# A two-layer graph network: the message stage's end reordered, eight source columns fetched row by row, and three scatters of the sum stage stored row by row

## What is computed

```
# layer 0: attention over the incoming edges, 4 heads of 32
h = relu(layernorm(x)); e = (h @ W_embed)
logit = leaky(dot_src[src] + dot_dst[dst]);  prob = softmax of logit over the edges with one dst
x = x + segment_sum(e[src] * prob, dst) + h @ W_lin + bias
# layer 1: messages, summed at the SOURCE node
h = relu(layernorm(x))
m = relu([h[src], h[dst], edge_attr] @ W1 + b1) @ W2 + b2
x = x + segment_sum(m * sigmoid(edge_attr @ Wa + ba), src)
```

## Time and profile before

| | us |
|---|---|
| median of 3 runs | 1634.91 |
| the profiled execution | 1633.1 |
| its span | 1631.4 |
| rows stage | 0 to 679 |
| sums stage | 679 to 985 |
| messages stage | 985 to 1631 |

### The profile page before, as it was taken

How to read it: one execution, slowest core, us unless ns; L and a number is a source line. 1 busy time by engine, 2 the same in 40 slices (tenths; PEclk the granted TensorE clock), 3 DMA queues, 4 the chain that set the end, 5 groups by cost and what they waited for, 6 DMA issues and landing times.

```text
span 1631.4 us, 24533 instructions
## 1 busy us (share of the span) xinstructions
PE 1118.8 (69%) x6191; PEld 848.0 (52%) x6191; DVE 1168.5 (72%) x3895; ACT 775.7 (48%) x2040; POOL 1105.6 (68%) x985
## 2 busy tenths in 40 slices
PE   2577677677777777554446545977778798888864
PEld 1455455555555555444445443644556566556543
DVE  3777787777877877976878675865666687777752
ACT  2567777777777777554545441322222222222221
POOL 6266666666666663266666656778788888888875
PEclk9988988988888888666756756998999999999988
DMA  4366666665666665454545442333333333333332
GB/s 125 105 203 193 200 194 194 213 194 190 212 197 200 199 199 163 137 155 146 161 132 162 144 133 66 47 54 52 53 53 53 52 52 54 53 51 51 54 48 28
DMA packets 181797, 202.75 MB, mean 124 GB/s; under 512 B 24777, under 2 KB 134225, under 8 KB 181657
## 3 DMA queue, kind: packets, MB, share of 16 engines
q1 hardware_dynamic: 123711, 129.49, 24.5%
q0 software_dynamic: 56272, 71.16, 22.2%
q10 hardware_dynamic: 1674, 0.53, 0.2%
HBM read 90.62 MB, written 109.66 MB: 123 GB/s over the span
## 4 chain that ended last, share of the span: by engine, by line
DVE 33%; SPq 23%; issue 15%; PE 12%; another core or an unknown queue 9%; ACT 3%; POOL 3%; DMA 1%; ACTq 1%; DVEq 0%; POOLq 0%
SPq L1254 15%; DVE st L540 4%; DVE BD L578 4%; SPq L1252 4%; SPq L1253 3%; DVE H L972 3%; DVE st L545 3%; PE bank L854 2%; PE bank L870 2%; PE bank L867 2%; DVE BD L585 2%; DVE BD L554 2%; DVE BD L1017 2%; PE bank L873 2%
## 5 line engine op out<-in xcount | busy, mean ns | idle before, releaser
L1194 POOL DMA_INDIRECT out_dram<-BD,BS x196 | 203.9, 1040 | 144.9 <-DVE BD L1021 88.9
L1274 POOL DMA_INDIRECT XE<-out_dram,gidx x189 | 187.2, 991 | 60.5 <-issue 54.3
L1141 PE MATMUL bank<-BD 128*128 128x128 f32 x392 | 115.2, 389 | 139.4 <-DVE BD L1017 80.7
L1288 POOL DMA_INDIRECT out_dram<-BS,sx x100 | 159.4, 1594 | 46.3 <-issue 37.6
L793 ACT ACTIVATE BD<-BD,nmr,rstd 128x128 f32<-128x128 f32 x392 | 171.0, 486 | 38.4 <-DVE nmr L561 28.9
L854 PE MATMUL bank<-ident,BD 128*128 128x128 f32 x588 | 121.7, 320 | 98.0 <-DVE BD L554 83.1
L1288 POOL DMA_INDIRECT out_dram<-TS,sx x96 | 153.1, 1595 | 34.4 <-issue 28.7
L1141 PEld LDWEIGHTS bank<-BD 128*128 128x128 f32 x392 | 91.0, 286 | 151.7 <-issue 151.7
L870 PE MATMUL bank<-wls,TS 128*128 128x128 f32 x784 | 142.4, 312 | 29.1 <-ACT TS L804 29.1
L867 PE MATMUL bank<-wes,TS 128*128 128x132 f32 x392 | 110.3, 368 | 72.8 <-issue 36.8
L182 POOL DMA_INDIRECT XE<-in_x_dram,gidx x104 | 102.5, 986 | 84.3 <-DVE BD L578 52.7
(11 more groups left out here) (237 smaller groups left out, 3035.0 us busy)
## 6 DMA issues: line engine op xcount, KB each, us to landing
out_dram<-BD SPq DMA_DIRECT2D x96, 512.0 KB
BD<-out_dram SPq DMA_DIRECT2D x896, 0.5 KB
base_rows<-BD SPq DMA_DIRECT2D x49, 256.0 KB
BD<-base_rows SPq DMA_DIRECT2D x49, 256.0 KB
H<-BD SPq DMA_DIRECT2D x49, 256.0 KB
XN<-in_x_dram SPq DMA_DIRECT2D x13, 512.0 KB
BD<-bond_rows SPq DMA_DIRECT2D x49, 128.0 KB
bond_rows<-in_edge_attr_dram SPq DMA_DIRECT2D x50, 125.0 KB
```

Source lines behind the costliest of these rows:

```text
L1141: nc.tensor.matmul(ps[6][:, 0:D], DG[u][:, c, :], BS4[u][:, c, :], start=first, stop=final, skip_group_check=True)
L1194: pool.indirect_dma_start(out, bass.IndirectOffsetOnAxis(sidx[:, it * G4 + c:it * G4 + c + 1], 0), RO4[u][:, c, :], None, bounds_check=lim ...
L1274: pool.indirect_dma_start(XS4[u][:, c, :], None, halves, bass.IndirectOffsetOnAxis(gidx[:, j, 0:1], 0), bounds_check=None, oob_is_err=Fals ...
L1288: pool.indirect_dma_start(halves, bass.IndirectOffsetOnAxis(sx[:, (u + 1) % 4, c:c + 1], 0), UPD[u][:, c * D:(c + 1) * D], None, bounds_ch ...
```

## The change

In the messages stage ROWED becomes range(7, 47, 5): eight columns, each fetched over five turns. The index columns are multiplied by the bytes of a half row by VectorE in the sums stage, 32 of them are loaded at a time, and the register is given away to the address (`donate`) instead of being copied and multiplied. In the last turns, the sums of turn 47 are formed by PE ahead of the `flip` of turn 48, and ACT copies them out (`take_sums`) ahead of turn 48's hidden layer. The wait of the last `flip` and the order of `keys` change with that.

In the sums stage, the fourth column of turns 2, 17 and 32 (KEPT) is no longer scattered by POOL. SP copies it into a buffer of its own when it is ready (`keep`, one DMA of 128 KB) and then stores its 128 rows, 1,024 bytes each, by 128 DMAs spread over the following fifteen turns (8 or 9 a turn); a position with nothing to store goes to a spare row. The addresses are worked out by VectorE in the rows stage and brought into one partition by three small DMAs.

```diff
@@ scatter_rows
+                at = slice(KEPT[0] * G4 + G4 - 1, KEPT[-1] * G4 + G4, KEPT.step * G4)
+                idle, goal = off[:, 0:len(KEPT)], off[:, 8:8 + len(KEPT)]
+                link(nc.vector.tensor_scalar(idle, spare[:, 0:len(KEPT)], 0.5, -0.5, ALU.mult, ALU.add))
+                link(nc.vector.tensor_tensor(goal, key0[:, at], idle, ALU.subtract))
+                link(nc.vector.tensor_tensor(goal, goal, emask[:, at], ALU.mult))
+                link(nc.vector.tensor_tensor(goal, goal, idle, ALU.add))
+                nc.vector.tensor_scalar(kept_to[:, :], goal, float(4 * W), None, ALU.mult).then_inc(kept_ready, 1)
@@ sums_sync
+            rows_stored(sp, 3)
+            sp.wait_ge(kept_ready, 1)
...
+                for k in range(len(KEPT)):
+                    sp.dma_start(kept_at[:, k * P:(k + 1) * P], kept_to[:, k:k + 1]).then_inc(ld_kcol, 16)
+            def keep(it, u):
+                sp.wait_ge(sc_rows, it + 1)
+                if it == KEPT[2]:
+                    sp.wait_ge(sc_srows[0], 16 * P)
+                sp.dma_start(XK[KEPT.index(it) % 2], RO4[u][:, G4 - 1, :]).then_inc(sc_kept, 16)
+            def store_rows(it):
+                for k, n in enumerate(KEPT):
+                    turn = it - n - 1
...
+                    for r in range(P * turn // KEPT.step, P * (turn + 1) // KEPT.step):
+                        if r % 32 == 0:
+                            regs[:] = [sp.alloc_register(f"kept{k}_{r + m}") for m in range(32)]
+                            sp.load(regs, kept_at[:, k * P + r:k * P + r + 32])
+                        at = sp.snap(regs[r % 32], donate=True, min_val=0, max_val=(ROWS_OUT - 1) * 4 * W)
+                        sp.dma_start(oflat[:, bass.ds(at, 4 * W)], XK[k % 2][r:r + 1, :].bitcast(U8)).then_inc(sc_srows[k % 2], 16)
@@ body, behind the H3 store and load_base(sp, it + 4, u)
+                if it in KEPT:
+                    keep(it, u)
+                store_rows(it)
@@ sums_vector, before the buffer is written again
-                    dve.wait_ge(sc_done[u], 16 * G4 * k)
+                    dve.wait_ge(sc_done[u], scattered(u, k))
+                    if it - 4 in KEPT:
+                        dve.wait_ge(sc_kept, 16 * (KEPT.index(it - 4) + 1))
@@ sums_gpsimd
+                    if it in KEPT and c == G4 - 1:
+                        continue
@@ messages: the rows of SP
-        ROWED = range(9, ITS - 2, 6)
+        ROWED = range(7, ITS - 2, 5)
-        LOADED = 16
+        LOADED = 32
-                        row = sp.snap(regs[r % LOADED], min_val=0, max_val=2 * (N - 1))
-                        sp.dma_start(XR2[k % 2][r:r + 1, :], halves[bass.ds(row, 1), :]).then_inc(ld_r[k % 2], 16)
+                        at = sp.snap(regs[r % LOADED], donate=True, min_val=0, max_val=2 * (N - 1) * ROWB)
+                        sp.dma_start(XR2[k % 2][r:r + 1, :].bitcast(U8), flat[:, bass.ds(at, ROWB)]).then_inc(ld_r[k % 2], 16)
@@ messages_scalar, body (take_sums waits for ms_sum and copies to UPD)
+                if it == ITS - 2:
+                    take_sums(it, u, k)
                 if upto(it, ITS - 2):
                     take_hidden(it + 1)
...
+                if it > 0 and it != ITS - 2:
+                    take_sums(it, u, k)
@@ messages_tensor, body (sums holds what stood here: the waits and line 1558's products)
+                if it != ITS - 2:
+                    sums(it, u, k)
...
+                if it == ITS - 3:
+                    keys(it + 2, u + 2, k + (u >= 2))
+                    flip_dst(it + 2, u)
+                    sums(it + 1, (u + 1) % 4, k + (u == 3))
+                    flip(it + 2, u + 2, k + (u >= 2))
```

More of the change, by code:

```diff
@@ L19 @@
 I32 = mybir.dt.int32
+U8 = mybir.dt.uint8
 ALU = mybir.AluOpType
@@ L471, in edge_turns, with scattered, sums_scattered @@
             return it // 4 + (it % 4 >= AHEAD)
+        KEPT = range(2, 33, 15)
+        kept_to = sb("kept_to", [P, len(KEPT)], I32)
+        kept_ready = sem("sc_kept_ready")
+        def scattered(u, k):
+            return 16 * sum(not (4 * m + u in KEPT and c == G4 - 1) for m in range(k) for c in range(G4))
+        def sums_scattered(eng):
+            for u in range(4):
+                eng.wait_ge(sc_done[u], scattered(u, ITS // 4 + (u == 0)))
+            for n in range(2):
+                eng.wait_ge(sc_srows[n], 16 * P * len(KEPT[n::2]))
         def rows_stored(eng, *slots):
@@ L911, in gnn_program @@
         sc_gathers = sem("sc_gather_indices")
+        kept_at = BD[0:1, 11136:11136 + len(KEPT) * P].bitcast(I32)
+        XK = [BD[:, 11648 + n * W:11648 + (n + 1) * W] for n in range(2)]
+        oflat = out.bitcast(U8).rearrange("n c -> (n c)").rearrange("(o c) -> o c", o=1)
+        ld_kcol, sc_kept = sem("sc_kept_offsets"), sem("sc_kept_rows")
+        sc_srows = [sem(f"sc_rows_stored{n}") for n in range(2)]
         FETCH = 4
@@ L923, in sums_sync @@
         def sums_sync(sp):
+            regs = []
+            rows_stored(sp, 3)
+            sp.wait_ge(kept_ready, 1)
+            with nc.allow_non_contiguous_dma(reason="one offset per partition"):
+                for k in range(len(KEPT)):
[8 more added lines that the diff above has]
+                    turn = it - n - 1
+                    if not 0 <= turn < KEPT.step:
+                        continue
+                    if turn == 0:
+                        sp.wait_ge(sc_kept, 16 * (k + 1))
+                        if k == 0:
+                            sp.wait_ge(ld_kcol, 16 * len(KEPT))
+                    for r in range(P * turn // KEPT.step, P * (turn + 1) // KEPT.step):
[4 more added lines that the diff above has]
+                        sp.dma_start(oflat[:, bass.ds(at, 4 * W)], XK[k % 2][r:r + 1, :].bitcast(U8)).then_inc(sc_srows[k % 2], 16)
             def body(it, u, k):
@@ L1027, in body @@
                     nc.vector.tensor_scalar(gsrc, gsrc, 2.0, None, ALU.mult).then_inc(sc_gathers, 1)
+                if it == WIDE + 2:
+                    first = blk(ROWED[-1]) * G4 + LANE
+                    dve.wait_ge(sc_gathers, 1)
+                    nc.vector.tensor_scalar(ocol[:, ::-1], gidx[:, first::G4 * SPAN, 0][:, 0:len(ROWED)], float(ROWB), None,
+                                            ALU.mult).then_inc(sc_gathers, 1)
                 if isinstance(it, int) and it == ITS - 4:
@@ L1199, in sums_gpsimd @@
                                     bounds_check=lim, oob_is_err=False).then_inc(sc_heads, 16)
-            for u in range(4):
-                pool.wait_ge(sc_done[u], 16 * G4 * (ITS // 4 + (u == 0)))
+            sums_scattered(pool)
             pool.wait_ge(sc_heads, 16)
@@ L1240, in messages_sync @@
         def messages_sync(sp):
-            regs = [sp.alloc_register(f"row{n}") for n in range(LOADED)]
+            regs = []
             def fetch_rows(it):
@@ L1448, in take_hidden, with take_sums @@
                 nc.scalar.activation(HID, bH[:, :], ACT.Relu, bias=b1c[:, 0:1]).then_inc(ms_hidr, 1)
+            def take_sums(it, u, k):
+                act.wait_ge(ms_sum, it + 1)
+                if past(k):
+                    act.wait_ge(ms_add, 16 * G4 * (it - 3))
+                nc.scalar.copy(UPD[u], bU[:, :]).then_inc(ms_upd, 1)
             def body(it, u, k):
@@ L1548, in body, with sums @@
                     hidden_src(it + 1)
+                if it != ITS - 2:
+                    sums(it, u, k)
+                if it == 0:
+                    flip_dst(1, 1)
+                    flip(1, 1, 0)
+                if it == 0 or isinstance(it, int) and it == ITS - 2:
+                    hidden_known(it + 1)
+                    hidden_src(it + 1)
+                if upto(it, ITS - 2):
+                    messages(it + 1)
+                if it == ITS - 3:
[3 more added lines that the diff above has]
+                    flip(it + 2, u + 2, k + (u >= 2))
+                if upto(it, ITS - 4):
+                    k2 = k + (u >= 2)
+                    flip_dst(it + 2, u)
+                    flip(it + 2, u + 2, k2)
+                    keys(it + 2, u + 2, k2)
+            def sums(it, u, k):
                 pe.wait_ge(ms_scaled, it + 1)
@@ L1561, in body @@
                 last.then_inc(ms_sum, 1)
[L1562 to L1574, removed]
             keys(0, 0, 0)
```

24 lines of the change are left out of this document (11 added, 13 removed).

## The result

The changed kernel takes **1666.55 us** (median of five, 1662.39 to 1673.51) against 1634.91 of the kernel before on the same chip: a ratio of 1.0192, 95% interval 1.0162 to 1.0221. The forecast was 1636, its range ended at 1658. What came is rival (A): the sums stage became SP's.

What follows compares the result with a forecast made beforehand. POOL bounds the messages stage, SP being as full; POOL and VectorE alternate in the sums stage. 1633.1 - 1.7 - 0.2 + 5.4 - 2 + 0.6 = 1635.2, about 1637 with the median's 1.8; halfway 1636 us, range 1621 to 1658.

Steps and rivals of the forecast that it cites:

- rival (A): Sums stage becomes SP's: each stored row costs 0.55 us or more; about 1651 at 0.6, 1687 at 0.69; chance 0.15.
- SP in the sums stage: SP's added copies, loads and 384 row stores, at 0.34 us a row, fit its waiting time: 0 us.
- cover of 19 us: Sums stage: SP's copy and base load are wanted about three turns later, so 19 us of delay would be absorbed.
- The end: Last turns of the messages stage: turn 47's sums moved ahead shorten POOL's wait from 4.31 to 2.65 us; -1.7 us.
- Three scatters: Sums stage: three scatters fewer save POOL 4.0 us at most, half of it taken; -2 us.
- VectorE's wait for the copies: Sums stage: VectorE's new wait for SP's copy has four turns (25 us) to be met.
- Small things: Rows stage: five small chained VectorE operations add 0.6 us; an eighth index DMA and the scaled indices add 0.
- Eighth column: Messages stage: one more column without a gather saves POOL a little; -0.2 us, bounds 0 to 1.3.
- Messages stream: Messages stage: SP, with 1,024 rows to fetch instead of 896, is 19 us late at turn 42; +5.4 us.
- Rival (B): Messages stage falls further behind SP, with turns of 14.5 us and over: 1646 to 1655 us; chance 0.1.
- (C): Messages stage: a fetched row's price stays 0.42 us, the copy or multiplication returning as another instruction; about 1710 us; chance 0.03.
- (D): More is gained than counted, the missing scatters also sparing waits between VectorE and POOL; about 1616 us; chance 0.07.

Runs made afterwards that it cites:

- e6: The changed kernel with POOL issuing only one of the four scatters in each turn of the sums stage; 1583.28 us.
- e1: The changed kernel with no column kept aside, all scatters left to POOL; 1633.55 us, 0.9971 of the kernel before.
- e3: The changed kernel without the 384 row stores and their 12 register loads, copies and waits staying; 1626.33 us, 0.9943 of the kernel before.
- e18: The changed kernel, unchanged, run again beside the kernel before; 1662.00 us, 1.0172 of the kernel before.

## Why the prediction was wrong

*The failed step* is "SP in the sums stage": I gave 0 us by taking "the fast price, since the sums stage's DMAs issued at an even 0.60 and 0.63 and the slow spells of the messages stage go with POOL's gathers, of which there are none here". Its two halves:

The price was 0.574 us, not 0.34. The slow spells go with POOL's indirect DMAs, scatters too (e6). I read the absence of a gather as an absence of the cause. Two DMAs a turn at an even 0.60 and 0.63 could not show a slow spell, for in one the base load takes 0.71 us (at 746.66), hardly more. A row of 0.23 us shows it. My own average of the fetches, 0.63 "with everything", was the better guide, and I had it among the arguments of rival (A).

The cover of 19 us was not there for the whole length. Here is the base load of turn 4 and that of turn 44, the last:

```profile
709.59 0.63 SPq L437 DMA_DIRECT2D BD<-base_rows  x1
...
990.62 0.61 SPq L437 DMA_DIRECT2D BD<-base_rows  x1
```

281.0 us for 40 turns, 7.03 each, where before they were 251.2 (697.69 to 948.87), 6.28 each. The last load came 41.75 us later than before and the stage ended 36.4 us later: 5.4 us of cover, not 19. In mid-stage SP copied and loaded 9 to 19 us, mostly 14 to 18, behind POOL's first scatter of the same turn, close to the 19, but turn 44's load came 8.9 us behind it: what still has to be done after the last base load can shrink by little (34.7 us before, 29.4 after), and a load that is late there is late at the end.

Rival (A) is thus right in its mechanism, its place and its price of a row (0.55 us or more), but not in what it makes of them. By its own sum a row of 0.574 gives (8.53 x 0.574 + 0.62 + 1.28 - 6.25) x 45 = 25 us, less 19 of cover: 1636 + 6 = 1642. The cover was 13.6 less. From the first store to the last copy of H, 696.7 to 1011.6, the 11 register loads took 15.5 us, 0.34 a turn where 0.62 stood for loads and copies, -12.4. The rest of that time, 315 - 220.5 - 15.5 = 79 us or 1.75 a turn, was neither store nor load, where I had 1.28 for the two DMAs: +21.3. Some 5 us of it are waits. In e6, without slow spells, the same rest is 1.33 a turn besides SP's waits, so slow spells stretch what surrounds the stores as well. Together 1642 + 13.6 - 12.4 + 21.3 = 1664.5, beside the 1666.55 measured; as the terms come from the changed kernel's own trace, this tells where the time lies and tests nothing.

*The end*, -1.7: right in size (4.31 to 2.59) and in what is late next. *Three scatters*, -2: 3.4 us between the stages of e1 and e3, within what a stage varies. *VectorE's wait for the copies*, 0: right (e3). *Small things*, +0.6: the first scatter comes 0.23 us later (679.12 and 679.35), and it lay between 678.7 and 691.1 in all traces, so nothing can be told. *Eighth column*, -0.2: not tried by itself. *Messages stream*, +5.4: wrong in sign. I said slow spells "won't shorten by dropping an instruction"; a row fell by 0.14 us, not by 0.08. 25.6 rows at 0.374 are 9.6 us, and with loads of 1.7 and the bond load's 0.4 a turn is 11.7 us, under POOL's 12.7, where I had 14.1. The load's 2.1 us was right. Rival (B) is out, (C) too (no register operation is left but the move), and (D)'s gains did not show.

With the two traces' stages in place of the terms: 1634 + 36 (sums stage) - 3 (messages and end) = 1667.

## What to carry to other kernels

An engine that waits most of a stage still has a price list of its own: before giving it a few hundred small DMAs, multiply by the average that such DMAs cost beside the busiest neighbour (here 0.53 to 0.57 us, and what stands around them stretches too), not by the cleanest step in the trace. Count a prefetch's lead as cover for a single stall; a stage that runs slow to its end gets back only the part of the lead that is left at the last transfer. To free 4 us of one engine, 230 us of another is a bad trade unless it is spread thin: 2.8 stores a turn cost at most a few us, 8.5 cost 36, and neither gained.

## What the hardware showed

Row DMAs of SP took 0.32 to 0.34 us each in fast spells and 0.7 to 1.4 in slow ones. The slow spells come with POOL's indirect scatters: 0.574 us a store with four scatters a turn (0.529 in e18), 0.324 with one. Bytes do not matter here (0.574 with 1,024 and with 64). The Trainium skill, "DMA: Bandwidth & Descriptors", Rules for kernel authors, says that small transfers pay overhead rather than bytes; the trace agrees in that. The 2 us that the prediction took from the Trainium skill, from the Anatomy section of the same page, are stated there for DMAs that POOL issues, and as a time to completion; these are SP's, and what counted was their issue. In a slow spell moves between registers, which are no DMAs, took up to 0.72 us as well, which I had not expected. A register load of 32 took 2.12 us, of one 0.488.
